# Metaformer block on one core: second norm shared among three engines, last rounds and the way to the router reordered

## The reference

```python
x = x + conv(ln_c(x))            # ln_c: over channels, eps 1e-6
t = tokens(x)                    # 16 x 1024 tokens x 128
t = t + ffn(ln_t(t))             # ln_t: over channels, eps 1e-5
# conv: q, k, v = w_qkv @ x; k = softmax(k, over pixels)
#   out = w_out @ ((k v^T)^T q) + b_out, in 8 heads of 32
# ffn(x): feat = mean(x, over the 16 images)
#   w = softmax(feat @ Wr + br)  # 1024 x 8, one for all images
#   h = relu(bn(x @ W1 + b1)); h = relu(bn(h @ W2 + b2))
#   y = h @ Wo + bo;  sum over the 8 experts of y * w
```

## Time and profile before

| what | value |
|---|---|
| median of 3 runs | 787.63 us (786.6 to 787.77) |
| the profiled execution | 788.47 us, span 786.7 us |
| PE busy | 765.5 us, 97% of the span |
| POOL busy | 641.7 us, 82% |
| DVE busy | 532.0 us, 68% |
| ACT busy | 438.4 us, 56% |

### The profile page before, as it was taken

The page is one execution under the profiler, slowest core; times in us unless marked ns, Lnnn a source line. Parts: engine busy times, 40 slices in busy tenths (PEclk is TensorE's granted clock), DMA queues, the critical chain, the costliest instruction groups (busy, mean ns, idle before and its releaser), DMA issues.

```text
span 786.7 us, 11860 instructions
## 1 busy us (share of the span) xinstructions
PE 765.5 (97%) x3863; PEld 624.9 (79%) x3863; DVE 532.0 (68%) x907; ACT 438.4 (56%) x610; POOL 641.7 (82%) x406
## 2 busy tenths in 40 slices
...
GB/s 223 106 171 155 191 139 185 149 173 216 108 136 28 200 72 135 16 119 92 41 133 4 130 75 58 133 0 133 83 50 133 0 133 67 66 134 1 54 27 28
DMA packets 27264, 80.60 MB, mean 102 GB/s; under 512 B 3120, under 2 KB 8152, under 8 KB 27232
## 3 DMA queue, kind: packets, MB, share of 16 engines
...
...
## 4 chain that ended last, share of the span: by engine, by line
PE 88%; DVE 7%; ACT 2%; issue 1%; POOL 1%; DMA 0%; POOLq 0%; DVEq 0%; SPq 0%; ACTq 0%
PE psum L615 65%; PE psum L605 6%; PE psum L579 5%; PE psum L560 3%; PE psum L593 3%; PE psum L511 1%; DVE st L1099 1%; DVE rawmax L1136 1%; PE psum L502 1%; PE psum L513 1%; PE psum L512 1%; DVE terms L1124 1%; DVE terms L1120 1%; PE psum L460 1%; DMA route_all<-in_x 0%
## 5 line engine op out<-in xcount | busy, mean ns | idle before, releaser
L1146 DVE SCALAR_TENSOR_TENSOR h_lo<-psum,h_hi 128x1024 fp32r<-128x1024 f32 x128 | 156.8, 1225 | 191.4 <-ACT h_hi L912 191.4
L912 ACT ACTIVATE h_hi<-psum 128x1024 fp32r<-128x1024 f32 x128 | 131.4, 1026 | 236.7 <-PE psum L615 236.7
L1383 POOL TENSOR_TENSOR h_lo<-w_raw,h_hi 128x1024 fp32r<-128x1024 f32 x64 | 154.6, 2418 | 40.0 <-ACT h_hi L931 40.0
L615 PE MATMUL psum<-h_hi,w_hi 128*128 128x512 f32 x382 | 119.8, 395 | 1.1 <-ACT route_all L924 1.1
L1167 DVE SCALAR_TENSOR_TENSOR w_raw<-psum,minus_t,route_all 128x1024 f32<-128x1024 f32 x93 | 118.6, 1276 | 2.3 <-POOL h_lo L1383 2.3
L615 PE MATMUL psum<-h_hi,w_lo 128*128 128x512 f32 x382 | 119.9, 395 | 0.0
L615 PE MATMUL psum<-h_lo,w_hi 128*128 128x512 f32 x382 | 118.9, 393 | 0.0
L1383 POOL TENSOR_TENSOR xn_lo<-feat_most,xn_hi 128x1024 fp32r<-128x1024 f32 x31 | 75.1, 2421 | 33.9 <-ACT xn_hi L931 33.9
L615 PEld LDWEIGHTS psum<-h_lo,w_hi 128*128 128x128 f32 x382 | 72.3, 189 | 16.6
L615 PEld LDWEIGHTS psum<-h_hi,w_hi 128*128 128x128 f32 x382 | 71.8, 189 | 16.9 <-ACT route_all L924 1.3
L615 PEld LDWEIGHTS psum<-h_hi,w_lo 128*128 128x128 f32 x382 | 72.3, 189 | 15.8
...
## 6 DMA issues: line engine op xcount, KB each, us to landing
...
```

What stands on the lines that cost most here:

```text
L615: mm = pe.matmul(dst[:, px], w[:, which, e, :], part[:, px], start=first and w is w_hi and part is hi, stop=last and part is lo, skip_grou ...
L912: nc.scalar.activation(h1_hi[r][:], z1[r] if src is None else src, ACT.Relu).then_inc(h1_hi_done, 1)
L1146: nc.vector.scalar_tensor_tensor(out=h1_lo[r][:], in0=z1[r] if src is None else src, scalar=0.0, in1=h1_hi[r][:].bitcast(F32), op0=ALU.max ...
L1383: nc.gpsimd.tensor_tensor(h2_lo[r][:], h2w[r], h2_hi[r][:].bitcast(F32), ALU.subtract).then_inc(h2_lo_done, 1)
```

## The change

In the rounds, the second norm gives ACT two chunks of each image (four from image 9 on), at the end of the step, and POOL the rest; for images 9 to 11 the rest is DVE's. The third `turn_e` stands ahead of `add_m`. POOL waits for DVE's variances right ahead of `scale_x`. In round 14 DVE's `statistics` stands ahead of mT_lo, and POOL's first split waits for xn_lo. In round 15 the transposes of x1 of image 14 go between the second and third `add_g`. Behind the rounds PE's parts are reordered: M ahead of the second half of layer 1, `add_m` ahead of layer 2, the logits ahead of layer 1 of expert 4. The norms of images 13 and 15 go to a second tile (`spare_norm`), feat is transposed with 14 images, and the norms of images 14 and 15 are transposed and added apart. The diff, cut, with eight columns of indentation taken off where all have them:

```diff
@@ -217,9 @@
-def norm2_split(image):
-    return 4 if isinstance(image, int) and image >= SHARED else 0
+def scalar_share(image):
+    return 4 if isinstance(image, int) and image >= SHARED else 2
@@ -257,6 @@
 x1_tokens = [x1T[:], w_raw[:, 2]]
+last_tokens, spare_norm = as_tokens(5), as_tokens(4)
@@ -461,6 @@
         turn_e(t, 1)
+        turn_e(t, 2)
         if at(t, IMAGES - 1):
@@ -468,7 @@
             add_m(q)
-        turn_e(t, 2)
         if at(t, 0):
@@ -477,8 @@
             turn_x(3, 3, 1)
-        for i in range(1, 4):
-            add_g(t, r, i)
+        add_g(t, r, 1)
+        if at(t, IMAGES - 1):
+            pe.wait_ge(x1_done, IMAGES - 1)
+            turn(p_chan, lambda n: x_res[0][:, 128 * n:128 * (n + 1)]).then_inc(x1t_done, 1)
+        add_g(t, r, 2)
+        add_g(t, r, 3)
         turn_rows(t, r, p_e)
@@ -700,24 @@
-    pe.wait_ge(h1_lo_done, 1)
-    turn(p_tok, lambda n: x_res[0][:, 128 * n:128 * (n + 1)]).then_inc(x1t_done, 1)
     pe.wait_ge(g_moved, IMAGES)
     heads_out()
-    pe.wait_ge(x1_done, IMAGES - 1)
+    pe.wait_ge(h1_lo_done, 1)
     half_layer1(p_k, 1, 0)
-    half_layer1(p_k, 1, 1).then_inc(l1_done, 1)
     pe.wait_ge(y_moved, IMAGES)
-    turn_rows(IMAGES, 0, p_g)
     for j in range(2):
...
     mm.then_inc(m_done, 1)
+    half_layer1(p_k, 1, 1).then_inc(l1_done, 1)
     pe.wait_ge(copy2_done, IMAGES - 1)
-    half_layer2(0)
     pe.wait_ge(m_lo_done, IMAGES)
     add_m(1)
+    turn_rows(IMAGES, 0, p_g)
+    half_layer2(0)
     half_layer2(1).then_inc(l2_done, 1)
     pe.wait_ge(x1_done, IMAGES)
+    pe.wait_ge(rows_moved, IMAGES + 2)
     turn(p_late, lambda n: x_res[1][:, 128 * n:128 * (n + 1)]).then_inc(x1t_done, 1)
@@ -725,29 @@
-    pe.wait_ge(feat_done, IMAGES - 1)
-    turn(p_chan, lambda n: feat[:, n, :]).then_inc(turned, 1)
+    pe.wait_ge(feat_done, IMAGES - 2)
     pe.wait_ge(rows_moved, IMAGES + 3)
+    turn(p_late, lambda n: feat[:, n, :]).then_inc(turned, 1)
+    pe.wait_ge(norm2_middle, 1)
+    pe.wait_ge(norm2_last, IMAGES - 1)
+    turn(p_chan, lambda n: xn2T[:, n, :]).then_inc(last_turned, 1)
+    layer2(2, 2)
+    pe.wait_ge(norm2_first, IMAGES - 1)
+    pe.wait_ge(norm2_middle, 2)
+    pe.wait_ge(norm2_last, IMAGES)
+    pe.wait_ge(feat_moved, 1)
+    turn(p_chan, lambda n: spare_norm[:, n, :]).then_inc(last_turned, 1)
+    pe.wait_ge(feat_most_moved, 1)
     layer1_into(p_late, 3)
-    layer2(2, 2)
-    pe.wait_ge(feat_most_moved, 1)
-    pe.wait_ge(norm2_first, IMAGES - SHARED)
-    pe.wait_ge(norm2_middle, 1)
-    pe.wait_ge(norm2_last, IMAGES)
-    turn(p_chan, lambda n: xn2T[:, n, :]).then_inc(last_turned, 1)
+    pe.wait_ge(feat_moved, 2)
+    for n in range(CHUNKS):
+        mm = pe.matmul(p_chan[:, EXPERTS * n:EXPERTS * (n + 1)], featT[:, 128 * n:128 * (n + 1)], wr_sb[:], start=True, stop=True)
+    mm.then_inc(logits_done, 1)
+    turn_rows(IMAGES + 2, 2, p_chan[:, BANK:PIXELS])
     pe.wait_ge(h1_lo_done, 3)
     layer1_into(p_k, 4)
-    pe.wait_ge(h1_lo_done, 4)
-    pe.wait_ge(feat_moved, 1)
-    for n in range(CHUNKS):
-        mm = pe.matmul(p_late[:, EXPERTS * n:EXPERTS * (n + 1)], featT[:, 128 * n:128 * (n + 1)], wr_sb[:], start=True, stop=True)
-    mm.then_inc(logits_done, 1)
-    turn_rows(IMAGES + 2, 2, p_g)
     layer2(3, 3)
...
-    pe.wait_ge(rows_moved, IMAGES + 4)
+    pe.wait_ge(h1_lo_done, 4)
     turn(p_late, lambda n: route[:, 0, n:n + 1].to_broadcast([128, 128])).then_inc(spread, 1)
@@ -756,6 @@
     pe.wait_ge(routeT_loaded, 16)
+    pe.wait_ge(rows_moved, IMAGES + 4)
     for n in range(2):
@@ -817,11 @@
             h1_high(0, 0, p_k)
-            norm2_high(t - 3, q)
         if a and not at(t, 0):
...
         move_e(t, r, 2)
+        if at(t, IMAGES - 1):
+            norm2_high(t - 3, r, x1_tokens[q], xn2T)
         move_e(t, r, 3)
+        if at(t, IMAGES - 1):
+            act.wait_ge(x1t_done, IMAGES - 1)
+            act.wait_ge(norm2_first, IMAGES - 3)
+            act.wait_ge(norm2_last, IMAGES - 3)
+            nc.scalar.copy(x1T[:], p_chan.rearrange("p (n c) -> p n c", c=C)).then_inc(copy2_done, 1)
         if at(t, 0):
@@ -833,8 @@
             expert_weights_high(1)
-        if isinstance(t, int) and SHARED <= t - 3 < IMAGES - 4:
-            norm2_high(t - 3, q)
+        if d and not at(t, IMAGES - 1):
+            norm2_high(t - 3, r, x1_tokens[q], xn2T)
@@ -847,13 @@
-    def norm2_high(image, q):
+    def norm2_high(image, k, tokens, out):
         act.wait_ge(ln_done, image + 6)
-        act.wait_ge(feat_done, image)
-        k = (image + 3) % 4
-        for n in range(norm2_split(image)):
-            ins = nc.scalar.activation(xn2T[:, n, :], x1_tokens[q][:, n, :], ACT.Identity,
+        wait(act, feat_done, image if out is xn2T else 0)
+        for n in range(scalar_share(image)):
+            ins = nc.scalar.activation(out[:, n, :], tokens[:, n, :], ACT.Identity,
                                        bias=norms[:, k, SHIFT, 1, n:n + 1], scale=norms[:, k, RSTD, 1, n:n + 1])
@@ -950,40 @@
     move_rows(IMAGES, 0, p_e)
-    act.wait_ge(x1t_done, IMAGES - 1)
-    act.wait_ge(norm2_first, IMAGES - 3 - SHARED)
-    act.wait_ge(norm2_last, IMAGES - 3)
-    nc.scalar.copy(x1T[:], p_tok).then_inc(copy2_done, 1)
+    norm2_high(IMAGES - 3, 0, x1_tokens[1], spare_norm)
     act.wait_ge(m_done, IMAGES)
-    move_rows(IMAGES + 1, 1, p_g)
     act.wait_ge(mx_done, IMAGES - 1)
     nc.scalar.copy(mT_hi[:], p_g[:, 256:384]).then_inc(m_hi_done, 1)
+    move_rows(IMAGES + 1, 1, p_g)
     h1_high(1, 1, p_k)
...
     act.wait_ge(x1t_done, IMAGES)
-    nc.scalar.copy(xT[:], p_late).then_inc(copy2_done, 1)
+    nc.scalar.copy(last_tokens, p_late.rearrange("p (n c) -> p n c", c=C)).then_inc(copy2_done, 1)
     z2_out(1)
...
     act.wait_ge(turned, 1)
-    nc.scalar.mul(feat_most[:], p_chan, 1.0 / IMAGES).then_inc(feat_most_moved, 1)
+    nc.scalar.mul(feat_most[:], p_late, 1.0 / IMAGES).then_inc(feat_most_moved, 1)
     act.wait_ge(ln_done, IMAGES + 5)
-    act.wait_ge(feat_done, IMAGES - 1)
-    for n in range(norm2_split(IMAGES - 1), MIDDLE):
-        ins = nc.scalar.activation(xn2T[:, n, :], xT[:, n, :], ACT.Identity,
+    act.wait_ge(feat_done, IMAGES - 2)
+    for n in range(3):
+        ins = nc.scalar.activation(spare_norm[:, n, :], last_tokens[:, n, :], ACT.Identity,
                                    bias=norms[:, 2, SHIFT, 1, n:n + 1], scale=norms[:, 2, RSTD, 1, n:n + 1])
-    ins.then_inc(norm2_middle, 1)
+    ins.then_inc(norm2_first, 1)
+    z2_out(2)
     h1_high(3, 3)
-    z2_out(2)
-    h1_high(4, 4)
-    first_xs_high(1)
     act.wait_ge(step_done, 3)
     nc.scalar.activation(grown[:].rearrange("p n e -> p (n e)"), shifted[:].rearrange("p n e -> p (n e)"), ACT.Exp).then_inc(grown_done, 1)
-    move_rows(IMAGES + 3, 1, p_g)
+    move_rows(IMAGES + 3, 1, p_chan[:, BANK:PIXELS])
+    h1_high(4, 4)
     act.wait_ge(routeT_done, 1)
...
     z2_out(3)
+    first_xs_high(1)
     keep_spread(2, p_tok)
@@ -1035,8 @@
             scale_weights(1)
-        if n:
-            statistics(t, slice(0, 2 if d else 1))
+        if n or at(t, IMAGES - 2):
+            statistics(t, slice(0 if n else 1, 2 if d else 1))
         if at(t, 0):
@@ -1047,7 @@
             nc.vector.tensor_tensor(mT_lo[:], p_g[:, 256:384], mT_hi[:].bitcast(F32), ALU.subtract).then_inc(m_lo_done, 1)
-        if not n:
+        if at(t, IMAGES - 1):
             statistics(t, OF_X1)
@@ -1062,10 @@
             halves(0, x_tokens[(r + 3) % 4], t + 3)
+        if isinstance(t, int) and IMAGES - 4 <= t < IMAGES - 1:
+            norm2_part(t - 3, r, x1_tokens[q], xn2T, range(4, CHUNKS), norm2_last)
         if at(t, IMAGES - 1):
+            statistics(IMAGES, OF_X1)
             h1_low(0, 0, p_k)
-            statistics(IMAGES, OF_X1)
-            norm2_part(IMAGES - 3, x1_tokens[1])
@@ -1099,15 @@
-    def norm2_part(image, tokens):
-        k = (image + 3) % 4
+    def norm2_part(image, k, tokens, out, chunks, done):
         dve.wait_ge(ln_done, image + 6)
-        dve.wait_ge(feat_done, image)
-        for n in range(norm2_split(image)):
-            ins = nc.vector.tensor_scalar(xn2T[:, n, :], tokens[:, n, :], norms[:, k, RSTD, 1, n:n + 1],
+        dve.wait_ge(feat_done, min(image, IMAGES - 2))
+        for n in chunks:
+            ins = nc.vector.tensor_scalar(out[:, n, :], tokens[:, n, :], norms[:, k, RSTD, 1, n:n + 1],
                                           norms[:, k, SHIFT, 1, n:n + 1], ALU.mult, ALU.add)
-        ins.then_inc(norm2_first, 1)
+        ins.then_inc(done, 1)
@@ -1199,6 @@
+    halves_part(1, x1T, IMAGES - 2, 0, CHUNKS).then_inc(stats_done[1], 1)
     dve.wait_ge(exp_done, 2 * IMAGES)
@@ -1207,29 @@
     ins.then_inc(y_moved, 1)
-    halves_part(1, x1T, IMAGES - 2, 0, CHUNKS).then_inc(stats_done[1], 1)
+    statistics(IMAGES + 1, OF_X1)
     dve.wait_ge(m_hi_done, IMAGES)
     nc.vector.tensor_tensor(mT_lo[:], p_g[:, 256:384], mT_hi[:].bitcast(F32), ALU.subtract).then_inc(m_lo_done, 1)
-    statistics(IMAGES + 1, OF_X1)
```

(53 more changed lines are left out.)

1 line of the change is left out of this document (removed).

## The result

| kernel | median | ratio to the kernel before |
|---|---|---|
| before | 787.7 us (786.6 to 788.97, 4 runs) | |
| changed | 778.08 us (777.55 to 778.66, 4 runs) | 0.9881 [0.9867, 0.9895] |

The change takes 9.6 us, 1.2%, off the kernel. The forecast was 780.3 us, 7.3 us faster; the range 776.2 to 784.0 holds the result. The profiled span fell from 786.7 to 775.8 us. The 1.1 us between the two lie ahead of GpSimd's `scale_x` of round 3 (65.69 and 66.77 us), so they are not the change's. From there on the stretches that the last table uses agree to 0.1 us.

What follows compares the result with a forecast made beforehand. Lost time was put at 210 to 270 us: PE idle, half clock, DVE stalled beside GpSimd. Terms 2.2 - 2.1 + 0.3 + 1.9 + 1.6 + 0.6 + 4.1 - 0.3 = 8.3, less 1.0, gave 7.3: 780.3 us, range 776.2 to 784.0.

Steps and rivals of the forecast that it cites:

- steady rounds, turn and share: Rounds 1 to 11: third turn of E fills PE's gap ahead of M x, 2.2 us; sharing the second norm with ScalarE, 0.
- rounds 12 to 14 up to the last k: DVE's chunks stall beside GpSimd's full-tile operations, 0.9 us lost twice; covered mT_lo waits give 0.3 us.
- entry, idle time: Ahead of the last round's k: PE's wait of 1.86 us goes, 1.9 us gained, bounds 0.9 and 1.9.
- entry's clock and last round: Last round: 1.6 us from less half clock, 0.6 from add_g no longer waiting for ScalarE, less 0.3 of chunk stall.
- tail, with handings-over: Behind the rounds to route's transpose: reordering gains 4.1 us, less 1.0 for handings-over between engines.
- spreads: Behind the tail: h1_low(4) comes later relative to route and holds a spread, 0.3 us lost, bounds -1 and 0.
- rival 3: Steady rounds give nothing: the gap reappears ahead of add_g(2), held by the cycle of rows and scale_x; 782.5 us, chance 0.10.
- Rival 1: Rounds 12 to 14: DVE's chunks do not stall, 2.1 us more gained, 778.2 us; chance 0.20.
- the covered waits for mT_lo of rounds 13 and 14 give 0.3: Rounds 13 and 14: PE's waits for mT_lo, covered after the change, give 0.3 us.
- Rival 2: The clock stays low in places, with gaps of 1 to 1.7 us remaining; cost 1.6 to 3.3 us, 782.5; chance 0.18.
- ten handings-over between engines in the tail ... take 1.0: Tail: ten handings-over between engines, counted at nothing in its timeline, cost 0.1 us each, 1.0 off the gain.
- rival 4: Tail: DVE's softmax subtraction stalls beside GpSimd's scaling and shifting, up to 2.4 us, 782 us; chance 0.06.

Runs made afterwards that it cites:

- the changed kernel's second profile: The changed kernel unaltered, run and profiled once more on another group's chip: 778.31 us, ratio 0.9886 to the kernel before; profiled span 776.9 us.
- the filled wait: Kernel before, with sixteen PE matmuls whose results nobody reads in the 1.86 us ahead of the last round's k: 788.29 us, ratio 1.0008.
- the entry alone: Kernel before, with only round 14 changed: DVE's statistics ahead of mT_lo, GpSimd's first split behind xn_lo: 784.6 us, ratio 0.9964.

## Why the prediction was right, and where its sizes were off

The measured terms are from the profiles; with the changed kernel's second profile the sum closes: 1.93 - 0.51 + 1.86 + 2.2 + 4.4 + 0.1 = 10.0, less 0.16 of start (`scale_x` of round 3 at 66.77 instead of 66.61), is 9.8 us, the difference of the spans 786.7 and 776.9.

| term | forecast | measured |
|---|---|---|
| steady rounds, turn and share | 2.2 + 0 | 1.93 (scaling of x in round 3 to k of round 12: 109.22 to 107.29) |
| rounds 12 to 14 up to the last k | -1.8 + 0.3 | -0.51 |
| entry, idle time | 1.9 | 1.86 |
| entry's clock and last round | 1.6 + 0.6 - 0.3 | 2.2 (16.47 to 14.29) |
| tail, with handings-over | 4.1 - 1.0 | 4.4 (27.5 to 23.1) |
| spreads | -0.3 | 0.1 |

**Steady rounds.** The size was right and the attribution was not. The prediction gave all to the third turn and nothing to the share, and excluded a gain of the share by its bounds. By the medians, the turn alone gave 0 (788.12 against 787.8), the share alone 0.5 (with an interval from -0.2 to 1.4), both together 2.9; by the traces, from k of round 3 to k of round 12, 0.1, 0.7 and 1.7. The prediction had seen that the third `add_g` hangs on `scale_x`, but not that `scale_x` in turn hung on GpSimd's own sum through DVE's statistics (1.05 us in the earlier trace rows). Only the share opened this ring. So rival 3 was true of the turn alone, though what held it was this ring and not the cycle of rows. That 2.2 was met is in part luck: it was forecast for an edit that gives nothing by itself.

**The stall of DVE's chunks.** The mechanism, drawn from contention in the earlier trace rows, is shown: 3.15 us beside a full tile, 1.23 with that tile cut to 128 columns. Rival 1 falls. Its price was right as well, 1.02 and 0.69 us for the forecast's 0.9 and 0.9, and 0.3 in round 15: from the start of its k to the heads' product behind it are 14.75 us (212.63 to 227.38), and 14.43 with the chunks back at GpSimd (212.64 to 227.07). The Trainium skill (page "SBUF — State Buffer", section "Who interferes with whom") says of tensor_scalar that it can take the port pair which DVE shares with GpSimd, and that the engine which comes second then blocks fully. The rows beside a full tile agree, the tail's do not: beside GpSimd's own tensor_scalar chunks DVE's four took 1.11 us, no longer than the 1.10 of chunks with nothing beside them, where the rule read as it stands has one of the two block.

**The step that was mis-sized** is "the covered waits for mT_lo of rounds 13 and 14 give 0.3". In the trace of before PE waits there:

```profile
195.73 0.50 PE L511 MATMUL psum<-xn_hi,mT_hi 128*128 128x512 f32 x1 [0.77 <-DVE mT_lo L1049]
...
208.41 0.51 PE L511 MATMUL psum<-xn_hi,mT_hi 128*128 128x512 f32 x1 [0.30 <-DVE mT_lo L1049]
```

These 1.07 us are gone in the changed kernel, and with the stall taken away the three rounds are 1.25 us shorter than before. The prediction names neither row and took 0.3 for both.

**Entry and clock.** The idle time came out as forecast, 1.86 for 1.9 us. The clock gave 1.5 for the forecast's 1.6, by the filled wait (16.40 to 14.87), which also showed that idle time is what the clock answers to. The kernel with the entry alone gave 3.2 of the 3.5 us. Of the 2.2 us of the last round, 0.6 are ScalarE's wait of the earlier trace rows, which is gone, and 0.3 go off for the stall; the remaining 0.4 were not traced. Rival 2 fell: the waits that remain, 1.66, 1.30 and 1.02 us, left the clock at 1.00. Why these did not lower it and the 1.86 did, no run here shows.

**Tail.** The timeline worked out from durations was met closely. From the end of the last `add_g` (226.92) the prediction had norm2 done at 4.2, the second sum at 8.5, the last power at 14.4, three chunks at 16.1, PE's turn at 17.1, logits and rows at 20.5 and route's transpose at 23.4; measured 4.2, 8.5, 13.9, 15.8, 17.1, 20.5 and 23.1. The step "ten handings-over between engines in the tail ... take 1.0" was the mistake: no row prices a handing-over, the steps' times came out right without one, and the charge of 1.0 came on top. The stall in the softmax (rival 4) did not occur; its row over 64 numbers takes 0.22 us, as GpSimd's shift was through at 247.44, before it began at 248.12:

```profile
245.09 2.35 POOL L1379 TENSOR_TENSOR xs_in<-xs_in,rows 128x1024 f32<-128x1024 f32 x1
...
248.12 0.22 DVE L1250 TENSOR_TENSOR shifted<-logits,top 128x64 f32<-128x64 f32 x1
```

The two missed each other by 0.7 us, which is luck as much as design. The spreads' part behind route's transpose took as long as before.

So the forecast was 2.2 us too careful by the medians and 2.5 by the spans, mostly from two charges: 1.0 for handings-over and some 1.0 for waits for mT_lo that were read too small. The tail's steps and the last round add 0.3 each, the spreads 0.4; the steady rounds take off 0.3 and the later start 0.2.
